# Recurrence: the score products of three steps ahead before the products into the state

## The chip, the cores and the metric

The kernel runs on one core of one Trainium2 chip. The metric is the time of one execution on the device in microseconds (us), the median of the runs shown. One more execution was taken with a profile; all rows come from it.

## The reference

An input x of 8 sequences of 1024 tokens with 512 features passes a feed-forward block, an attention block and the same feed-forward block again. The change is in the middle of the attention block, the gated delta rule with 16 heads of 32 features:

```
q, k, v = silu(conv(x @ W + b))            # q and k normalised per head
alpha, beta = sigmoid(x @ Wa + ba), sigmoid(x @ Wb + bb)
for t in tokens:                           # per sequence and head, state S is 32x32
    Sk = S @ k_t
    S  = alpha_t * S + beta_t * outer(v_t - alpha_t * Sk, k_t)
    o_t = S @ q_t
```

After it come a norm per head, a gate and an output projection.

## The kernel before

Five phases run one after the other: feed-forward, the projections and convolutions of attention, the recurrence (`recurrence_phase`), the output of attention, feed-forward. Only the third is touched.

The recurrence takes a sequence in chunks of 32 tokens. Inside a chunk the token loop becomes small matrix products, among them an inverse of a triangular 32x32 matrix that is built by squaring. The 8 sequences are taken in 4 pairs. A step n is one chunk of one pair: 32 chunks times 4 pairs make 128 steps. The state of a pair is touched once in four steps.

Work of several steps overlaps. The engines' loops are written out by hand, each engine takes its own instructions strictly in order, and semaphores tie them together. In one pass with number n TensorE does nine stages. Each stage is a call of `per_head`, 64 products of 32x32 tiles (8 column groups times 4 heads, line 1211 for all of them), after its waits:

- `scores(n+2)`: k and q against k times beta, into `ps_scores`. Waits for the load `qk_pe`, for `kb` of GpSimd and for VectorE's reading of the scores before
- `inverse(n)`, into `ps_end`; waits for `f4_t` and `y2` of VectorE
- `from_state(n)`, into `ps_chain`; waits, among others, for `state_ready`, that is for `new_state(n-1)` of VectorE
- `a_square(n+2)`, into `ps_a`; waits for `a_in_t` (line 1067)
- `f_square(n+1)`, into `ps_f`
- `solve(n)`, into `ps_end`
- `blocks(n+2)`, into `ps_tg`
- `f_fourth(n+1)`, into `ps_f2` (the trace writes it as ps_f out of yf); waits for `yf`
- `into_state(n)`, into `ps_chain`; waits for `u` and `kwp` of ScalarE

The loop of TensorE goes back after each step. Those of VectorE, ScalarE, GpSimd and SyncE hold four steps (the four pairs) and go back once in four.

VectorE does in each step, in this order: `triangles(n+2)` (lines 1064, 1067, 1069), `inverse` (1075), `residual` (1081, 1086), `after_a` (1093, 1094), `after_f` (1101, 1102), `scans` (1047, 1052, 1055), `after_tg` (1111, 1113), `after_f2` (1119, 1123), `turn_state(n+1)` (1129) and `new_state(n)` (1134). Two of them matter most here. `triangles(n+2)` waits for `scores_done` and is the first of a pass; `new_state(n)` is the last and waits for `o_ready`:

```python
def new_state(n, p):
    dve.wait_ge(o_ready, n + 1)
```

`o_ready` comes from ScalarE's `output(n)` (line 1180), which copies the step's output out of `ps_chain` and waits for `wrote`, the end of `into_state(n)`. So new_state(n) can't be done before into_state(n) has been copied out, and the next triangles stand behind new_state on VectorE.

SyncE loads `qk_pe` for the next scores when `scores_done` tells that the last ones have read it; GpSimd makes the next `kb` after the same semaphore.

Of the kernel before, what the change touches and what calls it, by code (L numbers as in the profile page):

```python
# [863 lines left out]
def recurrence_phase(nc, tag, streams, masks_dram, o_all):  # L864

    with ExitStack() as ctx:
# [69 lines left out]
        @block.sync  # L936
        def _(sp):
            def load_in(p, c):
                sp.dma_start(inb[p][:].rearrange("p b s g i -> p b (s g i)"), chunk_rows(p, c)).then_inc(in_loaded[p], 16)

            def load_qk(p, c):
                sp.dma_start(qk_pe[:].rearrange("p b s g i -> p b (s g i)"),
                             chunk_rows(p, c)[:, :, 0:2 * KT * CH]).then_inc(qk_loaded, 16)

            sp.dma_start(masks[:], masks_dram).then_inc(masks_loaded, 16)
            load_in(0, 0)
            load_qk(0, 0)
            for p in range(1, PAIRS):
                load_in(p, 0)
            for m in (1, 2):  # L950
                sp.wait_ge(scores_done, m)
                load_qk(m, 0)

            with sp.Fori(0, NCH) as c:
                for p in range(PAIRS):
                    n = c * PAIRS + p
                    sp.wait_ge(scores_done, n + 3)
                    load_qk((p + 3) % PAIRS, (c + (p + 3) // PAIRS) % NCH)
                    sp.wait_ge(zt_ready, n + 1)
                    load_in(p, (c + 1) % NCH)  # L960
            for p in range(PAIRS):
                sp.wait_ge(in_loaded[p], 16 * (NCH + 1))
            sp.wait_ge(qk_loaded, 16 * (NCH * PAIRS + 3))
# [237 lines left out]
        @block.tensor  # L1201
        def _(pe):
            def per_head(out, lhs_t, rhs, done, firsts=(0,)):

                pe.sem_inc(pe_turns, 1)
                for g in range(G):
                    for h in range(HG):
                        rows = slice(h * HD, (h + 1) * HD)  # L1210
                        last = nc.tensor.matmul(out(rows, g), lhs_t(rows, g), rhs(rows, g), start=g in firsts,  # L1211
                                                stop=True, skip_group_check=True)
                last.then_inc(done, 1)

            def scores(m):
                pe.wait_ge(qk_loaded, 16 * (m + 1))
                pe.wait_ge(kb_ready, m + 1)
                if not isinstance(m, int) or m > 0:
                    pe.wait_ge(pt_ready, m)
                per_head(lambda r, g: ps_scores[r, g, :, :], lambda r, g: kb[r, g, :],  # L1220
                         lambda r, g: qk_pe[r, g // KT, :, g % KT, :], scores_done)

            def a_square(m):

                pe.wait_ge(aint_ready, m + 1)
                if not isinstance(m, int) or m > 0:
                    pe.wait_ge(g_ready, m)
                per_head(lambda r, g: ps_a[r, g, :, :], lambda r, g: a_in_t[r, g, :], lambda r, g: a_pair[r, :, g, :], a_squared)

            def blocks(m):  # L1230

                pe.wait_ge(a2t_ready, m + 1)
                pe.wait_ge(t2_ready, m + 1)
                pe.wait_ge(g_ready, m + 1)
                if not isinstance(m, int) or m > 0:
                    pe.wait_ge(tf_ready, m)
                per_head(lambda r, g: ps_tg[r, g, :, :], lambda r, g: a2_t[r, g, :], lambda r, g: tg[r, :, g, :], tg_done)

            def f_square(m):

                pe.wait_ge(ft_ready, m + 1)
                if not isinstance(m, int) or m > 0:
                    pe.wait_ge(f2_ready, m)
                per_head(lambda r, g: ps_f[r, g, :, :], lambda r, g: f_t[r, g, :], lambda r, g: tf[r, :, g, :], f_squared)

            def f_fourth(m):

                pe.wait_ge(y1_ready, m + 1)
                pe.wait_ge(f2_ready, m + 1)
                if not isinstance(m, int) or m > 0:  # L1250
                    pe.wait_ge(y2_ready, m)
                per_head(lambda r, g: ps_f2[r, g, :, :], lambda r, g: f2_t[r, g, :], lambda r, g: yf[r, :, g, :], f2_squared)

            def inverse(n):
                pe.wait_ge(f4t_ready, n + 1)
                pe.wait_ge(y2_ready, n + 1)
                pe.wait_ge(u_ready, n)
                per_head(lambda r, g: ps_end[r, g, 0, :], lambda r, g: f4_t[r, g, :], lambda r, g: y2[r, g, :], f4_done)

            def from_state(n):  # L1260
                pe.wait_ge(state_t_ready, n + 1)
                pe.wait_ge(gqk_ready, n + 1)
                pe.wait_ge(state_ready, n)
                per_head(lambda r, g: ps_chain[r, g, 1:3, :], lambda r, g: state_t[r, g, :], lambda r, g: gqk[r, :, g, :],
                         read_done, firsts=(0, KT))

            def solve(n):
                pe.wait_ge(z_ready, n + 1)
                pe.wait_ge(inv_ready, n + 1)
                per_head(lambda r, g: ps_end[r, g, 1, :], lambda r, g: inv_t[r, g, :], lambda r, g: z[r, g, :], solved)  # L1270

            def into_state(n):
                pe.wait_ge(u_ready, n + 1)
                pe.wait_ge(kwp_ready, n + 1)
                per_head(lambda r, g: ps_chain[r, g, 0:2, :], lambda r, g: u[r, g, :], lambda r, g: kwp[r, :, g, :], wrote,
                         firsts=())

            scores(0)
            a_square(0)
            blocks(0)  # L1280
            scores(1)
            a_square(1)
            f_square(0)
            blocks(1)
            f_fourth(0)
            with pe.Fori(0, NCH * PAIRS) as n:
                scores(n + 2)
                inverse(n)
                from_state(n)
                a_square(n + 2)  # L1290
                f_square(n + 1)
                solve(n)
                blocks(n + 2)
                f_fourth(n + 1)
                into_state(n)


# [281 lines left out]
```

## Time and profile before

| | us |
|---|---|
| median of 3 runs | 3901.26 (3889.39 to 3907.76) |
| the profiled execution, its own time | 3902.36 |
| its span in the trace | 3900.6 |
| the recurrence's steady steps, first and last line 1064 in them | 1910.17 to 2963.55 |
| PE busy in the span | 3465.9 (89%) |
| DVE busy in the span | 2899.4 (74%) |

PE is TensorE's products, PEld its weight loads, DVE is VectorE, ACT ScalarE, POOL GpSimd, SP SyncE. Products of TensorE overlap and their ends are modelled, so distances between stages are read from start to start of the weight loads. A row of the timeline gives start, length, engine, line, operation, tiles and count, and in brackets the engine's idle time before it and what ended it.

### The profile page before, as it was taken

How to read it: one execution, taken by the hardware profiler on the slowest of the kernel's cores; microseconds unless marked ns; L12 is line 12 of the kernel's file. 1: busy time of each engine (PE TensorE's matmuls, PEld its weight loads, DVE VectorE, ACT ScalarE, POOL GpSimd, SP SyncE). 2: the span in 40 equal slices, each digit the busy share in tenths (PEclk: the TensorE clock that was granted, in tenths of full speed). 3: DMA queues.
4: the chain of work that ended last, by engine and by line, in shares of the span. 5: the costliest groups of instructions: out<-in, count | busy, mean ns of one | idle time of the engine just before them, and what ended most of it. 6: DMA issues, size and time to landing. Idle time of an engine off the chain costs nothing. (4 is left out here: it accounts for less than half of the span.)

```text
span 3900.6 us, 191339 instructions
## 1 busy us (share of the span) xinstructions
PE 3465.9 (89%) x84240; PEld 2881.0 (74%) x84240; DVE 2899.4 (74%) x4629; ACT 1573.1 (40%) x2348; POOL 1761.1 (45%) x1712
## 2 busy tenths in 40 slices
PE   4999994899999999998799999999996774999999
PEld 3888883666666666666699999999995553788887
DVE  5667764677677677675799999999997664676675
ACT  2544551566566666565111111111112231445554
POOL 0233234354354354453687777777773000222332
PEclk9999997999999999999899999999997886999999
DMA  1221222212322312313333333333333443112221
GB/s 76 97 97 67 94 86 98 87 75 86 137 78 86 140 75 86 140 65 120 119 106 110 107 109 111 106 112 106 110 107 115 186 194 151 64 76 97 97 87 64
DMA packets 132962, 402.05 MB, mean 103 GB/s; under 512 B 8768, under 2 KB 42304, under 8 KB 108992
## 3 DMA queue, kind: packets, MB, share of 16 engines
q1 hardware_dynamic: 132928, 401.62, 29.0%
q8 instruction: 19, 0.31, 0.0%
q14 instruction: 15, 0.12, 0.0%
HBM read 250.59 MB, written 150.99 MB: 103 GB/s over the span
## 5 line engine op out<-in xcount | busy, mean ns | idle before, releaser
L261 POOL TENSOR_TENSOR ffn_out<-ffn_gate,ffn_xres 128x512 f32<-128x512 f32 x128 | 186.4, 1485 | 792.3 <-DVE ffn_gate L228 791.9
L573 DVE SCALAR_TENSOR_TENSOR ain_conv<-ain_padded,ain_taps,ain_conv 128x512 f32<-128x512 f32 x384 | 413.4, 1077 | 13.6
L1171 ACT ACTIVATE rec_yf<-rec_ps_f 128x256 f32<-128x256 f32 x129 | 49.5, 383 | 638.7 <-DVE rec_f_t L1102 638.7
L989 POOL TENSOR_TENSOR rec_d_pair<-rec_dmat,rec_masks 128x512 f32<-128x512 f32 x131 | 205.7, 1570 | 203.8 <-DVE rec_dmat L1047 203.8
L665 POOL COPY ain_padded<-ain_tail 128x3 f32<-128x3 f32 x64 | 31.1, 486 | 552.3 <-ACT ain_conv L716 552.3
L675 POOL TENSOR_TENSOR ain_conv<-ain_conv,ain_term 128x512 f32<-128x512 f32 x192 | 267.9, 1395 | 16.0
L568 DVE COPY ain_padded<-ain_tail 128x3 f32<-128x3 f32 x128 | 82.3, 643 | 206.9 <-ACT ain_conv L716 206.9
L45 PE MATMUL ffn_ring<-ffn_mixkh,ffn_wkh 128*128 128x512 f32 x512 | 216.4, 423 | 0.0
L45 PE MATMUL ffn_ring<-ffn_mixrh,ffn_wrh 128*128 128x512 f32 x512 | 215.3, 421 | 0.0
L1211 PE MATMUL rec_ps_scores<-rec_qk_pe,rec_kb 32*32 32x64 f32 x8320 | 144.1, 217 | 72.6 <-issue 47.9
L725 ACT ACTIVATE ain_buf<-ain_conv 128x512 f32<-128x512 f32 x192 | 120.9, 630 | 217.0 <-POOL ain_conv L675 196.5
L45 PE MATMUL ffn_ring<-ffn_act_h,ffn_wvh 128*128 128x512 f32 x512 | 201.9, 394 | 0.0
L45 PE MATMUL ffn_ring<-ffn_mixrh,ffn_wrl 128*128 128x512 f32 x512 | 201.6, 394 | 0.0
L45 PE MATMUL ffn_ring<-ffn_mixkh,ffn_wkl 128*128 128x512 f32 x512 | 201.2, 393 | 0.0
L45 PE MATMUL ffn_ring<-ffn_act_h,ffn_wvl 128*128 128x512 f32 x512 | 200.8, 392 | 0.0
L45 PE MATMUL ffn_ring<-ffn_mixrl,ffn_wrh 128*128 128x512 f32 x512 | 199.7, 390 | 0.0
L45 PE MATMUL ffn_ring<-ffn_mixkl,ffn_wkh 128*128 128x512 f32 x512 | 199.7, 390 | 0.0
L45 PE MATMUL ffn_ring<-ffn_act_l,ffn_wvh 128*128 128x512 f32 x512 | 199.1, 389 | 0.0
L1211 PEld LDWEIGHTS rec_ps_scores<-rec_qk_pe,rec_kb 32*32 32x32 f32 x8320 | 126.9, 106 | 89.9 <-issue 89.9
L975 POOL TENSOR_TENSOR rec_decays<-rec_inb,rec_masks 128x512 f32<-128x512 f32 x131 | 166.7, 1272 | 32.4 <-DMA rec_inb<-streams 32.4
L177 DVE TENSOR_SCALAR ffn_var_tok<-ffn_mean 128x4 f32<-128x4 f32 x32 | 5.2, 162 | 229.8 <-PE ffn_mean L337 229.8
L672 POOL TENSOR_SCALAR ain_term<-ain_padded,ain_taps 128x512 f32<-128x512 f32 x192 | 155.5, 810 | 39.7 <-POOL ain_conv L675 26.4
(242 smaller groups left out, 10886.2 us busy)
## 6 DMA issues: line engine op xcount, KB each, us to landing
rec_inb<-streams SPq DMA_DIRECT2D x132, 640.0 KB, 4.0
streams<-ain_buf SPq DMA_DIRECT2D x16, 5120.0 KB, 15.6
rec_qk_pe<-streams SPq DMA_DIRECT2D x131, 256.0 KB, 2.7
ffn_x<-in_x SPq DMA_DIRECT2D x16, 1024.0 KB, 8.3
ffn_xres<-in_x SPq DMA_DIRECT2D x16, 1024.0 KB, 6.5
x<-ffn_out SPq DMA_DIRECT2D x16, 1024.0 KB, 4.6
ain_x<-x SPq DMA_DIRECT2D x16, 1024.0 KB, 11.9
gate<-ain_gate SPq DMA_DIRECT2D x16, 1024.0 KB, 3.9
```

What stands on the lines that cost most here:

```text
L45: last = nc.tensor.matmul(out, w[:, k, m * width:(m + 1) * width], x[:, k, :], start=(k == 0 and n == 0), stop=(k == KT - 1 and n == 2))
L261: last = nc.gpsimd.tensor_tensor(out[:, m, :], gate[:, m, :], xres[:, m, :], ALU.add)
L568: nc.vector.tensor_copy(pad[:, 0:TAPS - 1], tail[:, u, :]).then_inc(conv_step, 1)
L573: nc.vector.scalar_tensor_tensor(out=out[:], in0=pad[:, n:n + TOK], scalar=taps[:, u // KT, u % KT, n:n + 1], in1=out[:], op0=ALU.mult, op ...
L665: nc.gpsimd.tensor_copy(pad[:, 0:TAPS - 1], tail[:, u, :]).then_inc(pool_conv, 1)
L672: nc.gpsimd.tensor_scalar(term[:], pad[:, n:n + TOK], taps[:, u // KT, u % KT, n:n + 1], 1.0, ALU.mult, ALU.mult).then_inc(pool_conv, 1)
L675: nc.gpsimd.tensor_tensor(out[:], out[:], term[:], ALU.add).then_inc(pool_conv, 1)
L725: nc.scalar.activation(view, conv[u % 3][:].rearrange("p (c i) -> p c i", i=CH), ACT.Silu).then_inc(silued, 1)
L975: nc.gpsimd.tensor_tensor(decays[:].rearrange("p w (b f) -> p w b f", b=2), stream(s, NA).unsqueeze(1).to_broadcast([P, 2, 2, KT * CH]), m ...
L989: nc.gpsimd.tensor_tensor(d_pair[:], dmat[:].unsqueeze(1).to_broadcast(pair), masks[:, IN_BLOCK:OFF_BLOCK + 1, :].rearrange("p w (g i) -> ...
L1171: nc.scalar.activation(yf[:, 1], ps_f[:, :, 1, :], ACT.Copy).then_inc(f2_ready, 1)
L1211: last = nc.tensor.matmul(out(rows, g), lhs_t(rows, g), rhs(rows, g), start=g in firsts, stop=True, skip_group_check=True)
```

## The change

In a pass TensorE no longer begins with the scores of step n+2. It forms those of step n+3 after `f_fourth(n+1)` and in front of `into_state(n)`. The scores of step 2 move in front of the loop. No other engine's code is changed.

```diff
@@ -1283,8 +1283,8 @@
             f_square(0)
             blocks(1)
             f_fourth(0)
+            scores(2)
             with pe.Fori(0, NCH * PAIRS) as n:
-                scores(n + 2)
                 inverse(n)
                 from_state(n)
                 a_square(n + 2)
@@ -1292,6 +1292,7 @@
                 solve(n)
                 blocks(n + 2)
                 f_fourth(n + 1)
+                scores(n + 3)
                 into_state(n)
```

## Rows read from the trace of the kernel before

**Rows 1.** Busy time by stretch, one of ten alike in the recurrence.
```profile
core 0: us, PE busy (x) PEld busy (x) DVE busy (x) ACT busy (x) POOL busy (x), PEclk, DMA share, GB/s
2400.00:2500.00 100.00, 95.44 (x6831) 92.30 (x6824) 93.28 (x227) 18.73 (x48) 79.12 (x83) 1.00 0.35 110
```

**Rows 2.** Waits, 1900 to 2960 us: total, times, longest.
```profile
PE rec_ps_scores L1211 <- issue: 47.5, 126, 0.4
DVE rec_a_pair L1064 <- PE rec_ps_scores L1211: 44.1, 126, 0.6
DVE rec_state L1134 <- ACT o_all L1180: 0.3, 1, 0.3
```

**Rows 3.** Timeline, line 1064: near the first, four in the middle, the last.
```profile
1910.17 0.69 DVE L1064 TENSOR_TENSOR rec_a_pair<-rec_ps_scores,rec_d_pair 128x512 f32<-128x512 f32 x1 [0.27 <-PE rec_ps_scores L1211]
...
2323.00 0.69 DVE L1064 TENSOR_TENSOR rec_a_pair<-rec_ps_scores,rec_d_pair 128x512 f32<-128x512 f32 x1 [0.27 <-PE rec_ps_scores L1211]
...
2331.61 0.69 DVE L1064 TENSOR_TENSOR rec_a_pair<-rec_ps_scores,rec_d_pair 128x512 f32<-128x512 f32 x1 [0.50 <-PE rec_ps_scores L1211]
...
2339.97 0.69 DVE L1064 TENSOR_TENSOR rec_a_pair<-rec_ps_scores,rec_d_pair 128x512 f32<-128x512 f32 x1 [0.38 <-PE rec_ps_scores L1211]
...
2963.55 0.69 DVE L1064 TENSOR_TENSOR rec_a_pair<-rec_ps_scores,rec_d_pair 128x512 f32<-128x512 f32 x1 [0.27 <-PE rec_ps_scores L1211]
```

**Rows 4.** Timeline, weight loads of one plain step.
```profile
2414.65 0.96 PEld L1211 LDWEIGHTS rec_ps_scores<-rec_qk_pe,rec_kb 32*32 32x32 f32 x64 [0.49 <-issue]
...
2415.64 0.66 PEld L1211 LDWEIGHTS rec_ps_end<-rec_y,rec_f_t 32*32 32x32 f32 x64
...
2417.22 0.99 PEld L1211 LDWEIGHTS rec_ps_a<-rec_a_pair,rec_a_in_t 32*32 32x32 f32 x64
...
2418.12 0.99 PEld L1211 LDWEIGHTS rec_ps_f<-rec_tf,rec_f_t 32*32 32x32 f32 x64
...
2420.68 0.96 PEld L1211 LDWEIGHTS rec_ps_f<-rec_yf,rec_f_t 32*32 32x32 f32 x64
...
2421.55 0.99 PEld L1211 LDWEIGHTS rec_ps_chain<-rec_kwp,rec_u 32*32 32x32 f32 x64
...
2423.03 0.96 PEld L1211 LDWEIGHTS rec_ps_scores<-rec_qk_pe,rec_kb 32*32 32x32 f32 x64 [0.49 <-issue]
```

**Rows 5.** Timeline, VectorE and ScalarE in the same step.
```profile
2415.84 0.69 DVE L1064 TENSOR_TENSOR rec_a_pair<-rec_ps_scores,rec_d_pair 128x512 f32<-128x512 f32 x1 [0.27 <-PE rec_ps_scores L1211]
...
2416.56 0.45 DVE L1067 STREAM_TRANSPOSE rec_a_in_t<-rec_a_pair 128x256 f32<-128x256 f32 x1
...
2419.33 0.42 DVE L1101 TENSOR_TENSOR rec_yf<-rec_tf,rec_ps_f 128x256 f32<-128x256 f32 x1
...
2422.85 0.38 ACT L1180 ACTIVATE o_all<-rec_ps_chain 128x256 f32 x1 [2.04 <-PE rec_ps_chain L1211]
...
2422.91 0.38 DVE L1123 TENSOR_TENSOR rec_y<-rec_yf,rec_ps_f 128x256 f32<-128x256 f32 x1
...
2423.56 0.38 DVE L1134 TENSOR_TENSOR rec_state<-rec_s_decayed,rec_ps_chain 128x256 f32<-128x256 f32 x1
...
2424.21 0.69 DVE L1064 TENSOR_TENSOR rec_a_pair<-rec_ps_scores,rec_d_pair 128x512 f32<-128x512 f32 x1 [0.27 <-PE rec_ps_scores L1211]
```

**Rows 6.** Timeline where VectorE's loop goes back, ahead of 2331.61.
```profile
2330.01 0.38 ACT L1180 ACTIVATE o_all<-rec_ps_chain 128x256 f32 x1 [2.05 <-PE rec_ps_chain L1211]
...
2330.27 1.10 PE L1211 MATMUL rec_ps_scores<-rec_qk_pe,rec_kb 32*32 32x64 f32 x64 [0.41 <-issue]
...
2330.73 0.38 DVE L1134 TENSOR_TENSOR rec_state<-rec_s_decayed,rec_ps_chain 128x256 f32<-128x256 f32 x1
...
2332.34 0.45 DVE L1067 STREAM_TRANSPOSE rec_a_in_t<-rec_a_pair 128x256 f32<-128x256 f32 x1
...
2332.90 0.96 PEld L1211 LDWEIGHTS rec_ps_a<-rec_a_pair,rec_a_in_t 32*32 32x32 f32 x64
```

**Rows 7.** Timeline, the one step in which line 1134 waited for ScalarE.
```profile
1900.36 0.38 ACT L1180 ACTIVATE o_all<-rec_ps_chain 128x256 f32 x1 [4.52 <-PE rec_ps_chain L1211]
...
1900.78 0.42 DVE L1134 TENSOR_TENSOR rec_state<-rec_s_decayed,rec_ps_chain 128x256 f32<-128x256 f32 x1 [0.30 <-ACT o_all L1180]
```

## The prediction

> **What bounds the kernel now.** I read the busy time by stretch first. In the recurrence TensorE is busy 95 of 100 us and VectorE 93, at a granted clock of 1.00, the upper level of 2.4 GHz [rows 1]. Two engines so full leave no room for a reading by shares alone; what counts is who waits for whom in one step. The list of waits has three rows that matter [rows 2]. TensorE stands 0.4 us before every scores, and the releaser is "issue": nothing that the profile shows. VectorE stands some 0.35 us before every line 1064, for the scores. And line 1134, new_state, waits for ScalarE's copy only once in 126 steps. That last row is small, and the change aims straight at it.
>
> The starts of line 1064 give the pace: from 1910.17 to 2963.55 us there are 125 steps, so 8.43 us a step [rows 3]. It isn't even. Most steps take 8.38, but the one that ends at 2331.61 takes 8.61 and the next 8.36 [rows 3]. This long step returns every fourth time, where VectorE's loop goes back. Four steps take 4 x 8.427 = 33.71.
>
> Inside a plain step TensorE's stages follow each other without a hole, at about 0.9 us each, but from into_state to the next scores it takes 1.48 [rows 4]. A stage of this size takes 0.87 to 0.90 elsewhere, from f_fourth to into_state and from a_square to f_square [rows 4], so some 0.6 us are lost where TensorE's own loop goes back. VectorE, in turn, has an idle 0.27 before line 1064, which starts when the scores end [rows 5]. TensorE therefore sets the plain step; VectorE has a little slack.
>
> **The change part by part.** No arithmetic goes away in the loop. There is one scores stage more in all (131 for 130), at the very end: 0.9 us, unhidden, since into_state(127) stands behind it.
>
> The move takes away VectorE's wait for the scores: they are now ready before into_state starts. It puts 0.9 us between f_fourth(n+1) and into_state(n). Behind into_state hangs a queue: ScalarE's copy (line 1180), then new_state (1134), and, because VectorE takes its instructions in order, the next triangles (1064, 1067), whose transpose TensorE needs for a_square. In the kernel before, the copy started at 2422.85; line 1134 can start 0.42 after the copy's start, as the one step shows in which it did wait [rows 7], so it could have started at 2423.27 and did at 2423.56 [rows 5]. The slack is 0.29 us. The move asks for 0.87. So the slack is used up, and a ring closes that wasn't closed before.
>
> The ring, start to start:
> - line 1134 to 1064: two such steps on VectorE take 0.65 (1123 to 1134), so 0.33 [rows 5]
> - 1064 to 1067: 0.72 [rows 5]
> - 1067 to the weight loads of a_square, when these wait for it: 0.56 [rows 6]
> - a_square to into_state, in the order before: 2417.22 to 2421.55, 4.33 [rows 4]
> - the scores put in between: 0.87, as f_fourth to into_state; the upper bound is 0.99, scores to inverse [rows 4]
> - into_state to ScalarE's copy: 2421.55 to 2422.85, 1.30 [rows 4, 5]
> - copy to line 1134: 0.42 [rows 7]
>
> The sum is 8.53 us for a plain step, against 8.38. TensorE by itself would still do it in 8.38, so it now waits some 0.15 a step, and by its own order this shows in front of a_square: from f_square on, its own path gets there after 3.43 + 0.87 + 1.48 + 1.58 = 7.36 (f_square to into_state, scores, the way back to the loop's first stage, inverse to a_square [rows 4]); the other way, over copy and VectorE, takes 3.43 + 0.87 + 1.30 + 0.42 + 0.33 + 0.72 + 0.56 = 7.63. That is an idle of 0.27, of which the rest of the ring gives back about half.
>
> In the fourth step VectorE's loop goes back exactly between 1134 and 1064, inside the ring. Before, that was half hidden behind the scores: 1064 started at 2331.61, while the scores had ended at 2331.37 [rows 6]. Now nothing covers it. Its price has two bounds. From the start of 1134 to 1064 it took 2331.61 - 2330.73 = 0.88, which is 0.55 more than the plain 0.33 [rows 6]. But 1134 stood in line behind another instruction then; it was released 0.42 after the copy's start, at 2330.43. If the way back begins when 1134 is handed to the engine, it took 1.18, or 0.85 more. I take 0.85, because in that stretch VectorE ran without a gap, so that a way back that began early had work to hide behind and still showed. Nothing and less than nothing are excluded as a bound unless the engine's control can go on past a waiting 1134 (a rival, below).
>
> The Trainium skill prices such a way back lower: "Advanced Engine Details and Errata", section Control Flow Timing, gives about 51 ns for a branch and 108 ns for compare-and-branch. An estimate from that page would be 0.16 instead of 0.85, and the result 22 us lower. The gap of 0.50 idle in that step speaks against it [rows 3].
>
> Edits that cost nothing: kb and qk_pe of step n+3 are released by the end of the previous scores, nearly a whole step ahead, before and after; SyncE's load and GpSimd's product keep their place behind `scores_done` and have no other queue in front. Cover gone would cost their own wait, and then scores would show a wait for kb or a DMA. inverse(n+1), now the first of the pass, waits for y2: line 1123 ends at 2423.29, 5.17 after f_square started at 2418.12; inverse comes 3.43 + 0.87 + 1.48 = 5.78 after it [rows 4, 5]. No wait. f_fourth waits for line 1101's successor on ScalarE; 1101 starts 1.21 after f_square's loads in both orders [rows 4, 5], so nothing moves there.
>
> The sum: four steps take 4 x 8.53 + 0.85 = 34.97, which is 1.26 more than 33.71. There are 32 such fours: +40.3 us. With the last scores it is +41.2. On the profiled execution's own 3902.36 that makes 3943.6; this execution stands 1.1 above the median of 3901.26, so I say 3942.5.
>
> **The rivals.** Bounds: a measurement of this kernel can tell about 0.5% from no change, 19.5 us, so from 3881.8 to 3920.8.
>
> *The way back is hidden in the new wait.* If VectorE's control goes on past 1134 while this waits for the copy, the branch is done in the meantime. Then four steps take 34.12, +0.41, times 32 is 13, plus 0.9: 3915. For it: 1134 now waits, which it didn't before. Against it: the gap showed although the engine had queued work. The Trainium skill, same page, section Sequencer Loop, has the waits at the engine instruction with others read and queued meanwhile, which would lead to this case. 12%.
>
> *A longer ring.* The scores cost 0.99 rather than 0.87 in their new place: 0.12 x 128 = 15 more, 3958. For it: scores to inverse does take 0.99 [rows 4]; against: that was the first stage after the way back, the others take 0.9. 9%.
>
> *Nothing moves.* The wait for the scores was as long as the wait for the copy will be, and both engines keep their pace: 3902. It needs the ring to be 0.15 shorter in plain steps and the way back hidden. 5%.
>
> *Faster.* The hole of TensorE before scores is named "issue", not a loop. If it were something that only scores has to wait for, then it, and VectorE's 0.27 to 0.38 before 1064, vanish: a step loses about 0.27, 128 steps 35 us, 3867. The point that decides: copy and 1134 must come no later than now, so into_state must start no later although 0.87 of work stands before it; TensorE's order leaves only the hole of 0.6 to pay for that, and the slack of 0.29. 0.87 would just be paid. Against it: kb and the load are ready a step ahead. 4%.
>
> **How the numbers follow.** The forecast has 70%. The range goes from 3918, which takes in the lower bound of the way back (0.55: 34.67, +0.96 x 32 + 0.9 = +32, 3933), measuring noise and most of the way to the hidden case, to 3958, the longer ring. Slower by over 0.5%: 70 + 9 + 3 (of the hidden case, which stands near the bound): 82%. Within: 9 of it and 5: 14%. Faster: 4%.
>
> **What would show it.** In the changed profile: line 1134 waits for ScalarE in every step, 0.5 to 0.6 us; line 1064 no longer waits for the scores; TensorE has an idle before a_square (ps_a), released by line 1067, some 0.2 us, while its hole at the end of the pass stays, now before inverse. Starts of 1064 lie 8.53 apart, and 9.4 once in four. TensorE's share in the recurrence falls from 95 to about 92 of 100. The prediction is wrong if 1134 shows no wait, or if the fourth step isn't longer than the others.

## The result and the profile after

The changed kernel takes 3953.73 us (median of 4, 3947.34 to 3970.62), the kernel before 3898.60 in the same comparison. The ratio is 1.0148, with a 95% interval of 1.0114 to 1.0182: it became slower by 55 us, where 41 were forecast.

The waits of the recurrence, 1900 to 3000 us, in the changed kernel; columns as in [rows 2]:

```profile
DVE rec_state L1134 <- ACT o_all L1180: 83.8, 123, 3.1
...
PE rec_ps_chain L1211 <- DVE rec_state L1134: 35.6, 123, 0.3
PE rec_ps_end L1211 <- issue: 34.7, 124, 2.5
...
PE rec_ps_a L1211 <- DVE rec_a_in_t L1067: 9.5, 30, 0.4
DVE rec_a_pair L1064 <- issue: 9.3, 30, 0.3
```

Line 1134 now waits for the copy in every step, where it did so once before [rows 2], and line 1064 no longer waits for the scores. New is the second row: TensorE waits for line 1134 in front of a stage into ps_chain, which is from_state. The last two rows come in one step of four only, the long one.

One plain step in the timeline of the changed kernel:

```profile
2411.31 0.96 PEld L1211 LDWEIGHTS rec_ps_chain<-rec_gqk,rec_state_t 32*32 32x32 f32 x64 [0.37 <-issue]
...
2411.67 0.45 DVE L1067 STREAM_TRANSPOSE rec_a_in_t<-rec_a_pair 128x256 f32<-128x256 f32 x1
...
2412.32 0.96 PEld L1211 LDWEIGHTS rec_ps_a<-rec_a_pair,rec_a_in_t 32*32 32x32 f32 x64
...
2415.75 0.96 PEld L1211 LDWEIGHTS rec_ps_f<-rec_yf,rec_f_t 32*32 32x32 f32 x64
...
2416.78 0.96 PEld L1211 LDWEIGHTS rec_ps_scores<-rec_qk_pe,rec_kb 32*32 32x32 f32 x64
...
2417.64 0.99 PEld L1211 LDWEIGHTS rec_ps_chain<-rec_kwp,rec_u 32*32 32x32 f32 x64
...
2418.94 0.38 ACT L1180 ACTIVATE o_all<-rec_ps_chain 128x256 f32 x1 [3.07 <-PE rec_ps_chain L1211]
2419.03 0.66 PEld L1211 LDWEIGHTS rec_ps_end<-rec_y,rec_f_t 32*32 32x32 f32 x64 [0.39 <-issue]
...
2419.36 0.42 DVE L1134 TENSOR_TENSOR rec_state<-rec_s_decayed,rec_ps_chain 128x256 f32<-128x256 f32 x1 [0.65 <-ACT o_all L1180]
2419.70 0.68 DVE L1064 TENSOR_TENSOR rec_a_pair<-rec_ps_scores,rec_d_pair 128x512 f32<-128x512 f32 x1
2420.06 0.96 PEld L1211 LDWEIGHTS rec_ps_chain<-rec_gqk,rec_state_t 32*32 32x32 f32 x64 [0.37 <-issue]
```

From from_state to the next from_state it is 2420.06 - 2411.31 = 8.75, and the whole ring can be read off: from_state to a_square 1.01, to f_fourth 3.43, to the scores 1.03, to into_state 0.86, to the copy 1.30, to line 1134 0.42, to from_state 0.70. Together 8.75. Compare f_fourth to the next stage: 0.87 before [rows 4], 1.03 here.

Starts of line 1064, the first after the first full pass, three in the middle, and the last, with line 1134 ahead of the long step's:

```profile
1914.76 0.68 DVE L1064 TENSOR_TENSOR rec_a_pair<-rec_ps_scores,rec_d_pair 128x512 f32<-128x512 f32 x1
...
2322.11 0.68 DVE L1064 TENSOR_TENSOR rec_a_pair<-rec_ps_scores,rec_d_pair 128x512 f32<-128x512 f32 x1
...
2330.51 0.42 DVE L1134 TENSOR_TENSOR rec_state<-rec_s_decayed,rec_ps_chain 128x256 f32<-128x256 f32 x1 [0.65 <-ACT o_all L1180]
2331.24 0.69 DVE L1064 TENSOR_TENSOR rec_a_pair<-rec_ps_scores,rec_d_pair 128x512 f32<-128x512 f32 x1 [0.31 <-issue]
...
2366.69 0.69 DVE L1064 TENSOR_TENSOR rec_a_pair<-rec_ps_scores,rec_d_pair 128x512 f32<-128x512 f32 x1 [0.31 <-issue]
...
3031.02 0.68 DVE L1064 TENSOR_TENSOR rec_a_pair<-rec_ps_scores,rec_d_pair 128x512 f32<-128x512 f32 x1
```

The long step is 9.13 (2322.11 to 2331.24); in it line 1064 starts 0.73 after line 1134, where it does so after 0.34 in a plain step. Four steps, from one long one to the next, take 2366.69 - 2331.24 = 35.45, against 33.71 before: 1.74 more, times 32 is 56 us. That is the result, to a few us that come and go elsewhere. (This profiled execution has a span of 3968.9, the longest of the four; its phases ahead of the recurrence are 10.7 us longer than in the profile before, and no code differs there.)

TensorE is busy 92.4 of 100 us in the same stretch as [rows 1]:

```profile
2400.00:2500.00 100.00, 92.43 (x6481) 87.86 (x6473) 88.46 (x214) 18.08 (x46) 74.78 (x80) 1.00 0.34 104
```

The granted clock stays at 1.00, the level of 2.4 GHz, as before, so no part of the loss in these steps is the clock's.

### The profile page after: what moved, and what is told of

It is laid out like the page before. It is cut to its first block and busy times, and to the rows that moved or that the text cites. A ratio compares the mean times of both kernels' runs of the same rounds, so it can differ in the third digit from the quotient of the medians.

```text
span 3968.9 us, 191597 instructions
## 1 busy us (share of the span) xinstructions
PE 3502.7 (88%) x84304; PEld 2894.2 (73%) x84304; DVE 2890.0 (73%) x4629; ACT 1573.3 (40%) x2348; POOL 1771.4 (45%) x1712
## 5 line engine op out<-in xcount | busy, mean ns | idle before, releaser
L261 POOL TENSOR_TENSOR ffn_out<-ffn_gate,ffn_xres 128x512 f32<-128x512 f32 x128 | 217.0, 1726 | 791.4 <-DVE ffn_gate L228 791.0
L1180 ACT ACTIVATE o_all<-rec_ps_chain 128x256 f32 x128 | 49.2, 384 | 393.9 <-PE rec_ps_chain L1211 393.9
L1211 PE MATMUL rec_ps_chain<-rec_gqk,rec_state_t 32*32 32x64 f32 x8192 | 140.2, 215 | 36.8 <-DVE rec_state L1134 36.8
```

What stands on the lines that cost most here:

```text
L261: last = nc.gpsimd.tensor_tensor(out[:, m, :], gate[:, m, :], xres[:, m, :], ALU.add)
L1180: nc.scalar.activation(o_all[:, 2 * p:2 * p + 2, :, bass.ds(c * CH, CH)], ps_chain[:, :, 1, :].rearrange("p (b g) i -> p b g i", b=2), ACT ...
```

## The experiments

The changed kernel was not run again beside the experiments. The kernel before was, each time, and its median lay between 3895.02 and 3900.47; so two versions are best compared by their ratios to it, and a difference of their times can be off by some us.

The lists of the instructions as compiled show where the numbers are worked out that TensorE's waits compare with (n + 3 and the like, in registers). In the changed kernel the pass reads, stages by name:

```
(way back) ISA
inverse
from_state
REGISTER_ALU        # line 1225, a_square's n + 3
REGISTER_ALU        # line 1227, a_square's n + 2
a_square, f_square, solve, blocks, f_fourth
ISA                 # line 1216, 16 * (n + 4) for the load
scores
into_state
```

Before, an ISA and a REGISTER_ALU stood at the head, ahead of the scores, and a REGISTER_ALU between scores and inverse; none stood behind. A number is worked out where it is first used in the pass. The move thus carried arithmetic from the head into the ring, to the two places with a long distance: from_state to a_square (1.01) and f_fourth to scores (1.03). Whether it is the cause was tried in e2.

**e1, new_state ahead of the output.** Both read ps_chain, so the two were turned round and kept in order; leaving them unordered was not tried. (Parts of the edit; the places between them are left out.)

```diff
 def new_state(n, p):
-    dve.wait_ge(o_ready, n + 1)
+    dve.wait_ge(wrote, n + 1)
 def output(n, p, c):
-    act.wait_ge(wrote, n + 1)
+    act.wait_ge(state_ready, n + 1)
+act.sem_inc(o_ready, 1)             # ahead of ScalarE's loop
 def from_state(n):
-    pe.wait_ge(state_ready, n)
+    pe.wait_ge(o_ready, n + 1)
```

> The changed kernel, with new_state and ScalarE's output turned round: new_state waits for into_state itself and the output waits for new_state. Theory, that a ring over into_state, copy, new_state, from_state sets the step (8.75 us): the link from into_state to from_state shrinks from 1.30 + 0.42 + 0.70 = 2.42 to about 2.07, the ring falls to about 8.4, which TensorE needs anyway; the time comes down to 3895 to 3910, and line 1134 waits for PE. Rival, that the scores themselves cost more in their new place, whatever waits for into_state: the step stays near 8.75 and the time near 3950.

Measured: 3936.93, ratio 1.0100 (1.0084 to 1.0117). Timeline of e1:

```profile
2400.99 0.99 PEld L1212 LDWEIGHTS rec_ps_chain<-rec_kwp,rec_u 32*32 32x32 f32 x64
...
2402.20 0.42 DVE L1134 TENSOR_TENSOR rec_state<-rec_s_decayed,rec_ps_chain 128x256 f32<-128x256 f32 x1
...
2402.75 0.38 ACT L1180 ACTIVATE o_all<-rec_ps_chain 128x256 f32 x1 [3.52 <-DVE rec_state L1134]
...
2403.41 0.96 PEld L1212 LDWEIGHTS rec_ps_chain<-rec_gqk,rec_state_t 32*32 32x32 f32 x64 [0.37 <-issue]
```

The theory's shorter link did not come, and the rival's 3950 did not either. From into_state to from_state it takes 1.21 + 0.55 + 0.66 = 2.42, exactly as much as 1.30 + 0.42 + 0.70 in the other order: either order has one start of ScalarE and one of VectorE in it. The ring stayed, with a step of 8.71. What went is TensorE's long step. Starts of a_square, and line 1064 where VectorE's loop has gone back:

```profile
2308.58 0.96 PEld L1212 LDWEIGHTS rec_ps_a<-rec_a_pair,rec_a_in_t 32*32 32x32 f32 x64
...
2315.84 0.69 DVE L1064 TENSOR_TENSOR rec_a_pair<-rec_ps_scores,rec_d_pair 128x512 f32<-128x512 f32 x1 [0.31 <-issue]
...
2317.29 0.96 PEld L1212 LDWEIGHTS rec_ps_a<-rec_a_pair,rec_a_in_t 32*32 32x32 f32 x64
```

VectorE still has the way back between lines 1134 and 1064. But line 1134 now starts 1.21 after into_state instead of 1.72, so this branch has 0.5 us more room, and a_square comes every 8.71 (2317.29 - 2308.58), the long step too. Four steps take 4 x 8.71 = 34.84 instead of 35.45, 19.5 us in all; by the times it is 17, by the ratios 19.

**e2, numbers at the loop's head.**

```diff
 with pe.Fori(0, NCH * PAIRS) as n:
+    for value in (n + 3, n + 2, 16 * (n + 4), n + 4):
+        pe.compute_val(value)
     inverse(n)
```

> The changed kernel, with all numbers that TensorE's waits compare with worked out at the head of the loop; stages and waits are the same. Theory, that the move carried the arithmetic for these numbers out of the hole at the loop's head into the ring (0.15 from from_state to a_square, 0.15 before scores): f_fourth to scores falls from 1.02 to 0.88, from_state to a_square from 1.01 to about 0.9, where VectorE's path over line 1067 takes over; the step is about 8.5 and the time about 3922. Rival, that scores are slow to start there for another reason: both distances stay, 3950.

Measured: 3931.03, ratio 1.0092 (1.0075 to 1.0109), 23 us faster than the changed kernel, 22 by the ratios, where the expectation's 3922 meant some 30. Timeline of e2:

```profile
2399.64 0.45 DVE L1067 STREAM_TRANSPOSE rec_a_in_t<-rec_a_pair 128x256 f32<-128x256 f32 x1
...
2400.20 0.96 PEld L1211 LDWEIGHTS rec_ps_a<-rec_a_pair,rec_a_in_t 32*32 32x32 f32 x64
...
2403.62 0.96 PEld L1211 LDWEIGHTS rec_ps_f<-rec_yf,rec_f_t 32*32 32x32 f32 x64
...
2404.52 0.96 PEld L1211 LDWEIGHTS rec_ps_scores<-rec_qk_pe,rec_kb 32*32 32x32 f32 x64
```

f_fourth to scores is 0.90 instead of 1.03, and the shortest plain step 8.53 (others take up to 8.60). There a_square starts 0.56 after line 1067, so it waits for this line in every step, and no longer comes by from_state. The stages, waits and their order are those of the changed kernel, so the 0.2 us a step came from a few register instructions. They were not only moved: in the trace's records of TensorE's sequencer, which the views leave out, the changed kernel has one register instruction at the head and three in the ring, e2 a single one of 0.07 us at the head.

**e3, VectorE's loop cut at another place.**

```diff
+triangles(2, 2)
 with dve.Fori(0, NCH) as c:
     for p in range(PAIRS):
         n = c * PAIRS + p
-        triangles(n + 2, (p + 2) % PAIRS)
         inverse(n)
         ...
         new_state(n, p)
+        triangles(n + 3, (p + 3) % PAIRS)
```

> The changed kernel, with VectorE's loop cut at another place: triangles(n+3) at the end of a step instead of triangles(n+2) at its start, so the way back lies after line 1069 and out of the ring; VectorE's order is the same. Theory, that the way back costs about 0.45 in each fourth step because it lies in the ring: starts of line 1064 become even at 8.75, and the time falls by 32 x 0.4, about 13 us, to 3940. Rival, that it costs the same wherever it lies: no change, 3950.

Measured: 3947.49, ratio 1.0130 (1.0114 to 1.0147). Four starts of line 1064 in e3:

```profile
2308.84 0.68 DVE L1064 TENSOR_TENSOR rec_a_pair<-rec_ps_scores,rec_d_pair 128x512 f32<-128x512 f32 x1
...
2317.58 0.68 DVE L1064 TENSOR_TENSOR rec_a_pair<-rec_ps_scores,rec_d_pair 128x512 f32<-128x512 f32 x1
...
2326.39 0.68 DVE L1064 TENSOR_TENSOR rec_a_pair<-rec_ps_scores,rec_d_pair 128x512 f32<-128x512 f32 x1
...
2335.14 0.68 DVE L1064 TENSOR_TENSOR rec_a_pair<-rec_ps_scores,rec_d_pair 128x512 f32<-128x512 f32 x1
```

The steps are 8.74, 8.81 and 8.75; the long one of 9.13 is gone, four take 35.05. The trace shows the 0.4 in four. The times alone do not: 13 us were expected, 6 to 7 came, and the intervals overlap.

**e4, scores one stage earlier.**

```diff
-f_fourth(n + 1)
 scores(n + 3)
+f_fourth(n + 1)
 into_state(n)
```

> The changed kernel, with scores(n+3) one stage earlier, before f_fourth(n+1) instead of behind it. Theory, that any stage put between from_state and into_state lengthens the ring: a step as long as in the changed kernel, 8.75, and 3950 within 10 us. Rival, that what costs is only what stands right in front of into_state: the time goes back towards 3900.

Measured: 3954.74, ratio 1.0145 (1.0129 to 1.0162), as the changed kernel. One stage further from into_state the scores cost the same; as far as these two places show, what counts is that they stand between from_state and into_state.

**e5 and e6, the output's copy delayed,** in the kernel before and in the changed one, by a copy of `u` into a tile that nobody reads (its allocation isn't shown):

```diff
 def output(n, p, c):
     act.wait_ge(wrote, n + 1)
+    nc.scalar.activation(idle[:], u[:], ACT.Copy)
```

> The kernel before, with one more copy of a 128x256 tile (u into a tile that nobody reads) on ScalarE between into_state and the output, so that the output starts about 0.3 us later in each step. Theory, that into_state, copy and new_state had slack before: 0.29 at line 1134 and 0.3 more at line 1064, so nothing is lost; 3890 to 3905. Rival, that any delay of the copy costs in full: 128 x 0.3, 38 us more.

> The changed kernel with the same extra copy on ScalarE. Theory, that the ring over the copy sets the step: each step is longer by the whole 0.28 to 0.33, the time by 36 to 42 us, to about 3990. Rival, that the longer step comes from TensorE's own order and not from the ring: no change, 3950.

Measured: e5 3899.40, ratio 0.9998 (0.9988 to 1.0007); e6 3980.52, ratio 1.0209 (1.0192 to 1.0226). The same copy costs nothing before the change and 27 us after it, 24 by the ratios. Timeline of e5:

```profile
2409.19 0.99 PEld L1213 LDWEIGHTS rec_ps_chain<-rec_kwp,rec_u 32*32 32x32 f32 x64
...
2410.72 0.37 ACT L1182 ACTIVATE o_all<-rec_ps_chain 128x256 f32 x1
...
2411.21 0.38 DVE L1135 TENSOR_TENSOR rec_state<-rec_s_decayed,rec_ps_chain 128x256 f32<-128x256 f32 x1
```

Timeline of e6:

```profile
2404.65 0.99 PEld L1213 LDWEIGHTS rec_ps_chain<-rec_kwp,rec_u 32*32 32x32 f32 x64
2405.86 0.42 ACT L1181 ACTIVATE rec_idle<-rec_u 128x256 f32<-128x256 f32 x1 [2.89 <-PE rec_ps_chain L1213]
...
2406.19 0.37 ACT L1182 ACTIVATE o_all<-rec_ps_chain 128x256 f32 x1
...
2406.59 0.42 DVE L1135 TENSOR_TENSOR rec_state<-rec_s_decayed,rec_ps_chain 128x256 f32<-128x256 f32 x1 [0.92 <-ACT o_all L1182]
```

In e5 the output starts 1.53 after into_state instead of 1.30, and new_state 2.02 after it, where it was 2.01 [rows 4, 5]: the delay of 0.23 is within the slack of 0.29. In e6 the output is later by as much, and new_state starts 1.94 after into_state instead of 1.72: 0.22 a step, not the 0.28 to 0.33 of the expectation, and 128 x 0.22 = 28. The pair shows that the path over the copy had slack before and sets the step after. By which branch it comes back to TensorE, the timeline and e2 show.

**e7 and e10, the parts together in the changed kernel.** e7 has the edits of e1, e2 and e3, e10 those of e2 and e3.

> The changed kernel with three edits at once: the numbers worked out at the loop's head, VectorE's loop cut behind line 1069, and new_state before the output. The parts leave a ring of about 8.71 - 0.22 = 8.49 and no long step: four steps take 34.0 against 33.7 before, 3900 to 3912. Rival, that the parts hide each other and only one counts: 3925 or more.

> The changed kernel with the numbers worked out at the loop's head and VectorE's loop cut behind line 1069, the output before new_state as it was. Theory: the ring with the copy and new_state in their old order is as long as with them turned (2.42 both ways from into_state to from_state), so this is as fast as the version with all three edits: steps of 8.5, 3905 to 3918. Rival, that the turned order gave something of its own: 3920 or more.

Measured: e7 3908.43, ratio 1.0025 (1.0015 to 1.0034); e10 3918.67, ratio 1.0063 (1.0046 to 1.0080). The parts add up in e7. In e10 the theory misses, and the intervals of the two ratios don't meet: turning the two did give something of its own once the numbers were out of the way. Timeline of e10, then of e7:

```profile
2403.35 0.45 DVE L1067 STREAM_TRANSPOSE rec_a_in_t<-rec_a_pair 128x256 f32<-128x256 f32 x1
...
2403.91 0.96 PEld L1212 LDWEIGHTS rec_ps_a<-rec_a_pair,rec_a_in_t 32*32 32x32 f32 x64
```

```profile
2409.53 0.45 DVE L1067 STREAM_TRANSPOSE rec_a_in_t<-rec_a_pair 128x256 f32<-128x256 f32 x1
2409.63 0.96 PEld L1213 LDWEIGHTS rec_ps_chain<-rec_gqk,rec_state_t 32*32 32x32 f32 x64 [0.29 <-issue]
...
2410.50 0.99 PEld L1213 LDWEIGHTS rec_ps_a<-rec_a_pair,rec_a_in_t 32*32 32x32 f32 x64
```

In e10 a_square starts 0.56 after line 1067: the price of a waiting a_square that the prediction had read [rows 6]. In e7 it starts 0.97 after line 1067 and 0.87 after from_state, so it doesn't wait for line 1067. From line 1134 two branches lead to a_square, over from_state and over lines 1064 and 1067, and they are almost equally long. Without the register instructions the second is the longer; in e7, where line 1134 comes early, the first is again. Steps are 8.55 on average in e10 and 8.46 in e7.

**e8 and e9, the same two edits on the kernel before.** e8 has the numbers at the head (16 * (n + 3), n + 3, n + 2 and n + 1 here) and VectorE's loop cut elsewhere, with one more scores behind TensorE's loop, which the last triangles needs; e9 has the numbers alone.

> The kernel before (scores at the head of the pass), with the numbers worked out at the loop's head and VectorE's loop cut behind line 1069. Theory, that TensorE's own pass of 8.38 sets the step here: scores to inverse falls from 0.99 to about 0.87, part of which the longer head may take back, and the long fourth step goes (0.2 in four); 3875 to 3892. Rival, that the step is held by a ring as in the changed kernel: no change, 3898.

> The kernel before, only with the numbers worked out at the loop's head. Theory: of the 19 us that the two edits gave together, this one gives most, since TensorE's own pass falls from 8.38 to about 8.24 (0.14 x 128 = 18), while the long fourth step (0.2 in four, 32 x 0.2 = 7) stays and is felt more; 3882 to 3890. Rival, that VectorE's way back is what was gained: 3893 or more.

Measured: e8 3881.27, ratio 0.9951 (0.9935 to 0.9968); e9 3881.85, ratio 0.9964 (0.9953 to 0.9976). Both beat both kernels. Timeline of e9:

```profile
2401.36 0.96 PEld L1211 LDWEIGHTS rec_ps_scores<-rec_qk_pe,rec_kb 32*32 32x32 f32 x64 [0.42 <-issue]
...
2402.26 0.69 PEld L1211 LDWEIGHTS rec_ps_end<-rec_y,rec_f_t 32*32 32x32 f32 x64
```

Scores to inverse takes 0.90 instead of 0.99 [rows 4], and the head got no longer but shorter: 1.41 from into_state (2399.95 to 2401.36, its row isn't shown), against 1.48. The plain step is 8.24 in both. Most of the gain is the numbers', as expected. What e8's second edit adds is too little for the times to tell.

## Why the prediction was right, and where it wasn't

**Right: the mechanism.** The slack of 0.29 was overdrawn, a ring closed over into_state, the copy and new_state, and the step follows it. e5 and e6 show this directly, e4 shows that one stage earlier costs the same. Line 1134's wait (0.65, forecast 0.5 to 0.6), the vanished wait of line 1064, the longer fourth step and TensorE's share (92.4) came as said. The rivals "nothing moves" and "faster" are out.

**Out too: the hidden way back.** This rival needed VectorE's control to go on past a waiting line 1134. The records of VectorE's sequencer, which the views leave out, show the loop's first instruction on the way back 0.01 after the start of line 1134, in the 26 long steps of the changed kernel where it could be read (2330.53 in the step above). In all steps the sequencer's next record behind line 1134 stands 0.43 after the start of ScalarE's copy, in the kernel before and in the changed one alike: it comes when the copy has released line 1134, also where 1134 itself starts later.

**Mis-sized: the plain step, 8.53 forecast, 8.75 measured.** Three terms:
- "the scores put in between: 0.87" was 1.03. The bound of 0.99 that the rival "a longer ring" took was nearer. The reason that the prediction gave for these 0.99 (the first stage after the way back) was wrong: it is the arithmetic for the wait, which sits wherever the number is first used. e2 brings f_fourth to scores back to 0.90, and e9 scores to inverse, in its old place.
- The ring was closed over lines 1064 and 1067, at 0.33 + 0.72 + 0.56 = 1.61 from line 1134 to a_square. The measured branch goes over from_state: 0.70 + 1.01 = 1.71. The list of stages has from_state's wait for `state_ready`, but the prediction never worked out when from_state is released. Hence also the wrong place for TensorE's idle: it stands before from_state, before a_square only in the fourth step. That this branch became the longer one is the arithmetic again: two register instructions stand between from_state and a_square, which take 1.01 with them and 0.87 without (e7). In e2, with them out, a_square waits for line 1067, and the plain step is the 8.53 of the forecast.
- a_square to into_state without the scores was 4.29 instead of 4.33.

0.16 + 0.10 - 0.04 is the missing 0.22, times 128 some 28 us. The term that the sum lacked is thus the register instructions, which it put at nothing.

**Mis-sized the other way: VectorE's way back, 0.85 taken, about 0.4 measured** (line 1134 to 1064 takes 0.73 instead of 0.34). Four steps are longer by 0.45 than 4 x 8.75, but one of four takes 8.81 in e3 too, where the way back lies outside the ring, so some 0.06 are not its price. Even the lower bound of 0.55 was too high. Both bounds came from a stretch in which line 1064 also waited for the scores: by the sequencer's records the way back did begin at 2330.45, as the prediction had it, but from 2330.91 to 2331.43 VectorE waited for the scores, and these 0.5 were counted as way back. By the Trainium skill's branch times ("Advanced Engine Details and Errata", Control Flow Timing) an estimate was 0.16; the measured 0.4 is more, but a way back also holds register instructions that those two figures don't cover. The 0.45 instead of 0.85 gave back 13 us of the 28. That the forecast came within 14 us is in this part luck: two errors of opposite sign. The time of the rival "a longer ring", 3958, lies nearer to the measured 3953.73 than the forecast does.

**The rest.** The first pass of TensorE's loop is longer (line 1064 from 1896.16 to 1914.76, 18.6 us, against 15.99 before), 2.6 us that the prediction didn't have. That the change did this is not shown: e9, with the stages in their old order, took 19.66 there. The last scores' 0.9 was not measured by itself.

## What to carry to other kernels

A stage that only looks like filler between two others may lie on the way to a third engine's copy and back; before moving it, add up the ring from each of its waits, and over every branch, since here two differed by 0.1 us. Slack can be measured rather than guessed: put a useless instruction on the path in question and see whether the time moves. In a loop with short stages, look at where the numbers for the waits are worked out: with TensorE's pass as the bound, working them out together at the loop's head gave 0.36% for nothing.

## What the runs showed of the hardware that was not expected

- Register instructions between two stages of TensorE cost time, although the stage ahead of them has just handed over 64 products. One costs 0.09 to 0.13 us (scores to inverse 0.99 with it, 0.90 in e9 without; f_fourth to scores 1.03 and 0.90), two cost 0.14 (from_state to a_square 1.01, and 0.87 in e7).
- At the loop's head the numbers cost nothing that could be seen: into_state to the first stage took 1.48 before, 1.41 in e9, where all of them are worked out there. The sequencer's records have two register instructions of about 0.04 us each at the head before, and a single one of 0.06 in e9.
- VectorE's sequencer did not pass an instruction that still waited for a semaphore: in the changed kernel the way back began 0.01 after line 1134 had started, and never in the 0.65 in which it waited.
- ScalarE's first instruction starts 1.30 us after into_state's first weight load when it reads ps_chain. When it reads only the tile u it starts after 1.21 (e6), which is also what VectorE needs when it reads ps_chain (e1).
